# Causal grouped attention: the row maxima from the high halves alone, two heads at a time on rows 0-63 and 64-127 of the array, and the side work of a round placed anew

## What is computed

```python
q = (x @ wq).reshape(b, t, HQ, K)       # HQ = 16, K = V = 64
k = (x @ wk).reshape(b, t, HKV, K)      # HKV = 4, G = 4 query heads for each key head
v = (x @ wv).reshape(b, t, HKV, V)
q = q * cos + _neg_half(q) * sin
k = k * cos + _neg_half(k) * sin
qg = q.reshape(b, t, G, HKV, K)
scores = jnp.einsum('btghk,bThk->bghtT', qg, k)
scores = jnp.where(mask, scores, -jnp.inf) / np.float32(np.sqrt(K))
p = jax.nn.softmax(scores, axis=-1)
out = jnp.einsum('bghtT,bThv->btghv', p, v).reshape(b, t, HQ * V)
return out @ wo
```

## Time and profile before

| | us |
|---|---|
| median of 3 runs | 1379.15 (1377.59 to 1379.6) |
| the profiled execution | 1377.09 |
| its span, first to last instruction | 1375.3 |
| mean granted TensorE clock in the span | 0.921 |

### The profile page before, as it was taken

One profiled execution on the slowest core, in us unless ns is written; L12 is line 12 of the kernel. 1 busy time (PEld: TensorE's weight loads), 2 busy tenths in 40 slices (PEclk: granted clock), 3 DMA queues, 4 the chain that ended last, 5 costly groups with the idle time before them and its releaser, 6 DMA issues.

```text
span 1375.3 us, 35916 instructions
## 1 busy us (share of the span) xinstructions
PE 1123.1 (82%) x14984; PEld 841.2 (61%) x14984; DVE 1056.3 (77%) x2097; ACT 840.2 (61%) x1488; POOL 1000.7 (73%) x786
## 2 busy tenths in 40 slices
PE   4767776459999999999999999999999998610891
PEld 2666666126667676776676766767767676510781
DVE  5576665768889889888898898888988975583665
ACT  2644555258778787787787777877877886100230
POOL 2554567659888888898898888988988897317355
PEclk9999998579999999999999999999999999555896
DMA  6140001122122121122221211212212110013694
GB/s 210 41 142 1 1 2 68 41 88 52 54 67 49 50 74 37 51 59 55 59 52 46 74 36 54 57 55 58 52 47 48 36 26 1 1 35 116 193 301 153
DMA packets 49246, 90.84 MB, mean 66 GB/s; under 512 B 8896, under 2 KB 19136, under 8 KB 48832
## 3 DMA queue, kind: packets, MB, share of 16 engines
q1 hardware_dynamic: 46128, 81.21, 20.7%
q0 software_dynamic: 2960, 7.38, 1.9%
HBM read 43.96 MB, written 13.01 MB: 41 GB/s over the span
## 4 chain that ended last, share of the span: by engine, by line
PE 64%; DVE 19%; POOL 6%; issue 5%; SPq 3%; ACT 2%; DMA 1%; POOLq 0%; DVEq 0%
PE psT L1082 5%; PE psS L1152 5%; PE psS L1151 5%; PE psT L1070 5%; PE psS L1173 5%; PE psS L1174 5%; PE psS L1175 4%; PE psT L1100 3%; PE psO L1082 3%; PE psO L1152 3%; PE psO L1151 3%; POOL rows_in L708 2%; DVE pmax L1552 2%; DVE nmax L1401 2%; DVE psT L1529 2%
## 5 line engine op out<-in xcount | busy, mean ns | idle before, releaser
L682 POOL TENSOR_TENSOR probs<-arena,probs 128x512 f16<-128x512 f32 x576 | 652.3, 1157 | 113.5 <-ACT probs L866 113.1
L866 ACT ACTIVATE probs<-arena 128x512 f16<-128x512 f32 x576 | 358.0, 622 | 0.0
L874 ACT ACTIVATE arena<-psS 128x512 f32<-128x512 f32 x384 | 228.1, 594 | 144.7 <-PE psS L1155 82.4
L1173 PE MATMUL psS<-vb,probs 128*128 128x65 f16 x2304 | 301.9, 192 | 4.6 <-POOL probs L682 2.4
L1174 PE MATMUL psS<-vb,probs 128*128 128x64 f16 x2304 | 303.3, 194 | 0.0
L1175 PE MATMUL psS<-vb,probs 128*128 128x65 f16 x2304 | 301.4, 192 | 0.0
L1173 PEld LDWEIGHTS psS<-vb,probs 128*128 128x128 f16 x2304 | 220.0, 97 | 72.7 <-issue 9.4
L1174 PEld LDWEIGHTS psS<-vb,probs 128*128 128x128 f16 x2304 | 215.4, 97 | 47.4
L1552 DVE TENSOR_REDUCE pmax<-psT 128x1 f32<-128x512 f32 (+1 forms) x305 | 193.6, 639 | 39.7 <-PE psT L1082 19.0
L1175 PEld LDWEIGHTS psS<-vb,probs 128*128 128x128 f16 x2304 | 216.8, 98 | 0.0
L1152 PE MATMUL psS<-arena 65*128 65x512 f16 (+1 forms) x448 | 157.1, 351 | 0.0
(11 more groups left out here) (268 smaller groups left out, 2884.6 us busy)
## 6 DMA issues: line engine op xcount, KB each, us to landing
arena<-arena SPq DMA_DIRECT2D x240, 128.0 KB, 2.4
arena<-w_exp_dram SPq DMA_DIRECT2D x40, 384.0 KB, 4.2
arena<-xnT_d SPq DMA_DIRECT2D x16, 512.0 KB, 3.8
wkv<-w_d SPq DMA_DIRECT2D x16, 352.0 KB, 4.2
rows_in<-arena POOLq DMA_DIRECT2D x1, 2580.0 KB, 18.6
arena<-rows_in SPq DMA_DIRECT2D x40, 64.5 KB, 3.1
arena<-x_dram SPq DMA_DIRECT2D x4, 512.0 KB, 5.3
hres<-x_dram SPq DMA_DIRECT2D x4, 512.0 KB, 5.0
```

The lines of the kernel that those rows point to most:

```text
L682: pool.tensor_tensor(pl[:, r, :], pf[:, r, :], ph[:, r, :], ALU.subtract).then_inc(lo_P, 1)
L866: act.activation(ph[:, s % RING, :], pf[:, s % RING, :], ACT.Copy).then_inc(b_hi, 1)
L874: act.activation(pf[:, s % RING, :], score_banks[s % SCORES], ACT.Exp).then_inc(b_exp, 1)
L1173: pe.matmul(dst, high, vb[:, p, j, 0:OW], start=first, stop=False, skip_group_check=True)
```

## The change

The row maxima come from the high halves of q and k alone (K=64 instead of K=128). Two heads are done together: the matmul of head g reads qB and kB on partitions 0 to 63, that of head g+1 qA and kC on partitions 64 to 127, and they write two side banks; mask matmuls follow for both. So two "max" entries stand side by side in the list, and PE waits for both banks before it fills them. All maxima of heads 0 and 1 and five pairs for heads 2 and 3 are made in the round before, the other five pairs for heads 2 and 3 in steps 2 to 11 of the round. PROJ, OUTP, HIGH_AT, LOW_AT and the rows have new steps. The low halves of q for heads 0 and 1 count on a semaphore of their own (ql_in), for which scores of step 0 wait, no longer the maxima; qk_in therefore counts 112 a round. The first maxima of the next round's heads 2 and 3 (s = 31) wait for q1_in, which still counts all six copies. SP's order puts `spread_q(.., 0)` ahead of the rows, and there are two row semaphores. The prologue makes 30 maxima and two rows instead of 16 and one.

```diff
-EARLY = {4: (0,), 5: (1,), 6: (2,), 7: (3,), 8: (4, 5)}
-LATE = {0: (6,), 1: (7,), 2: (8,), 3: (9,)}
-ROW_AT = 5
+THIS_PAIR = {2: 5, 5: 6, 7: 7, 9: 8, 11: 9}
+NEXT_PAIR = {14: 0, 16: 1, 17: 2, 19: 3, 20: 4, 22: 5, 24: 6, 26: 7, 28: 8, 29: 9}
+LATER_PAIR = {31: 0, 32: 1, 33: 2, 34: 3, 35: 4}
+ROWS_AT = {13: 2, 15: 3, 31: 4, 33: 5}
...
-PROJ = {0: ("k", 0), 1: ("k", 1), 3: ("q", 0, 0), 5: ("r", 0, 0), 7: ("q", 0, 1), 9: ("r", 0, 1), 11: ("v",),
-        13: ("q", 1, 0), 15: ("r", 1, 0), 17: ("q", 1, 1), 19: ("r", 1, 1)}
-OUTP = {21: ("turn", 0), 23: ("turn", 1), 25: ("turn", 2), 27: ("turn", 3), 30: ("out", 0), 33: ("out", 1)}
-HIGH_AT = {4: 0, 12: 1, 22: 2}
-LOW_AT = {5: 0, 15: 1, 25: 2}
+PROJ = {0: ("k", 0), 1: ("k", 1), 3: ("q", 0, 0), 4: ("r", 0, 0), 6: ("q", 0, 1), 7: ("r", 0, 1), 9: ("v",),
+        16: ("q", 1, 0), 18: ("r", 1, 0), 21: ("q", 1, 1), 24: ("r", 1, 1)}
+OUTP = {11: ("turn", 0), 13: ("turn", 1), 15: ("turn", 2), 17: ("turn", 3), 20: ("out", 0), 23: ("out", 1)}
+HIGH_AT = {4: 0, 10: 1, 26: 2}
+LOW_AT = {5: 0, 11: 1, 27: 2}
...
+        if s in THIS_PAIR:
+            now += pair(2, THIS_PAIR[s])
+        if not last and s in NEXT_PAIR:
+            now += pair(G, NEXT_PAIR[s])
+        if not last and s in LATER_PAIR:
+            now += pair(G + 2, LATER_PAIR[s])
...
-                    sp.dma_start(qA[0:HD, p, 2 * c + h, :], qlo[HD * h:HD * h + HD, c, :]).then_inc(landed, 16)
+                    sp.dma_start(qA[0:HD, p, 2 * c + h, :], qlo[HD * h:HD * h + HD, c, :]).then_inc((ql_in, q1_in)[c], 16)
...
-                spread_row(row_of(1), p, 1)
                 if not last:
                     spread_k(it + 1, 1 - p)
+                    spread_q(it + 1, 1 - p, 0)
                 spread_row(row_of(2), p, 2)
-                if not last:
-                    spread_q(it + 1, 1 - p, 0)
                 spread_row(row_of(3), p, 3)
                 if not last:
                     spread_q(it + 1, 1 - p, 1)
                     spread_row(row_of(4), 1 - p, 0)
+                    spread_row(row_of(5), 1 - p, 1)
...
+            def fill_pair(e, banks, p, n):
+
+                g = e[1] % G
+                if g == 0 and e[2] == 0:
+                    pe.wait_ge(qk_in, 112 * n + 112)
+                if g == 2 and e[2] == 0:
+                    pe.wait_ge(q1_in, 96 * n + 96)
+                w = min(4, PIECES[e[2]][0][0] + 1 - 4 * PIECES[e[2]][0][1]) * P
+                done = []
+                for k, (i, h) in enumerate(PIECES[e[2]]):
+                    diag = h == i // 4
+                    mm = [pe.matmul(banks[0][:, k * w:(k + 1) * w], qB[0:HD, p, g, i * P:(i + 1) * P],
+                                    kB[0:HD, p, h * 512:h * 512 + w], start=True, stop=not diag),
+                          pe.matmul(banks[1][:, k * w:(k + 1) * w], qA[HD:P, p, g + 1, i * P:(i + 1) * P],
+                                    kC[HD:P, p, h * 512:h * 512 + w], start=True, stop=not diag)]
+                    if diag:
+                        mm = [pe.matmul(dst[:, (k + 1) * w - P:(k + 1) * w], identh[:, :], maskh[:, :],
+                                        start=False, stop=True) for dst in banks]
+                    done = mm
+                for mm in done:
+                    mm.then_inc(side_full, 1)
...
+                if e[0] == "max":
+                    before(entries, i + 1, base, prior)
+                    fill_pair(e, [side_banks[bank], side_banks[(i + 1) % SB]], (1 - p) if nxt else p, it + 1 if nxt else it)
+                    return
...
-                    pe.wait_ge(row_in, 16 * (it * G + g) + 16)
+                    pe.wait_ge(row_in[g % 2], 16 * (it * G + g) // 2 + (16 if g % 2 == 0 else 8))
+                if s == 0:
+                    pe.wait_ge(ql_in, 32 * it + 32)
```

More of the change, by code:

```diff
@@ L74, in reader, with pair @@
     return READER[entry[0]]
-PROJ = {0: ("k", 0), 1: ("k", 1), 3: ("q", 0, 0), 5: ("r", 0, 0), 7: ("q", 0, 1), 9: ("r", 0, 1), 11: ("v",),
-        13: ("q", 1, 0), 15: ("r", 1, 0), 17: ("q", 1, 1), 19: ("r", 1, 1)}
-OUTP = {21: ("turn", 0), 23: ("turn", 1), 25: ("turn", 2), 27: ("turn", 3), 30: ("out", 0), 33: ("out", 1)}
-HIGH_AT = {4: 0, 12: 1, 22: 2}
-LOW_AT = {5: 0, 15: 1, 25: 2}
+PROJ = {0: ("k", 0), 1: ("k", 1), 3: ("q", 0, 0), 4: ("r", 0, 0), 6: ("q", 0, 1), 7: ("r", 0, 1), 9: ("v",),
[3 more added lines that the diff above has]
+LOW_AT = {5: 0, 11: 1, 27: 2}
+def pair(h, n):
+    return [("max", h, n), ("max", h + 1, n)]
 def side_work(first, last):
@@ L88, in side_work @@
     for s in range(SPR):
-        h, c = divmod(s, SPH)
         now = []
[L91 to L94, removed]
+        if s in THIS_PAIR:
[4 more added lines that the diff above has]
+            now += pair(G + 2, LATER_PAIR[s])
         if not last and s in PROJ:
@@ L98, in side_work @@
             now.append(OUTP[s])
-        if c == ROW_AT and not (last and h == G - 1):
-            now.append(("row", h + 1))
+        if s in ROWS_AT and not (last and ROWS_AT[s] >= G):
+            now.append(("row", ROWS_AT[s]))
         steps.append(now)
@@ L106 @@
 SB = 3
-PROLOGUE = ([PROJ[s] for s in sorted(PROJ)] + [("max", G, n) for n in range(len(PIECES))] + [("row", G)]
-            + [("max", G + 1, n) for c in sorted(EARLY) for n in EARLY[c]])
+PROLOGUE = ([PROJ[s] for s in sorted(PROJ)] + [e for n in range(len(PIECES)) for e in pair(G, n)]
+            + [("row", G), ("row", G + 1)] + [e for s in sorted(LATER_PAIR) for e in pair(G + 2, LATER_PAIR[s])])
 PROLOGUE += [("gap",)] * (-len(PROLOGUE) % SB)
@@ L359, in build @@
         r_mul, r_hi, r_lo, qk_in = sem("rotated_parts"), sem("high_halves"), sem("low_halves"), sem("qk_in")
-        max_ready, row_in = sem("max_ready"), sem("row_in")
-        q1_in = sem("second_heads_in")
+        max_ready, row_in = sem("max_ready"), [sem("row_in0"), sem("row_in1")]
+        q1_in, ql_in = sem("second_heads_in"), sem("first_heads_low_in")
         b_hi, lo_P, v_hi = sem("high_probs"), sem("low_probs"), sem("high_values")
@@ L457, in spread_row @@
                 sp.dma_start(qB[HD:HD + 1, p, g, :].rearrange("o (i t) -> o i t", t=P),
-                             hrow[:, g % 2, :]).then_inc(row_in, 16)
+                             hrow[:, g % 2, :]).then_inc(row_in[g % 2], 16)
             for b in range(2, B):
@@ L482, in _ @@
             store_input2(2)
-            spread_row(start(0, "A"), 0, 0)
+            spread_row(1, 0, 0)
+            spread_row(2, 0, 1)
             store_input2(3)
@@ L1072, in fill @@
                     return mm
[L1073 to L1087, removed]
                 if kind == "row":
@@ L1123, in side @@
                 e = entries[i]
-                if e[0] == "gap":
+                if e[0] == "gap" or e[0] == "max" and e[1] % 2 == 1:
                     return
@@ L1196, in _ @@
                     pe.wait_ge(ones_set, 4)
-                if PROLOGUE[i] == ("max", G + 1, 0):
+                if PROLOGUE[i] == ("max", G + 2, 0):
                     pe.wait_ge(n2_T, 2)
```

## The result

The changed kernel takes 1546.7 us (median of 4 runs, 1545.47 to 1552.85) against 1378.37 us: a ratio of 1.1233, with a 95% interval of 1.1198 to 1.1268. The forecast was 1455 and the range ended at 1510: the direction was right, the size less than half of what came (+77 forecast, +168 measured).

The account below looks back on a forecast made before the run. PE's stream was taken to bound the old round; the new round, walked along DVE, was 59.0 us against 54.4. 1377.1 + 69 (fifteen rounds) + 10 (prologue) - 2 (last round) = 1454, median 1455, range 1385 to 1510.

Parts of the forecast that it names:

- The stalls: PE waiting for copies of q before the next round's first maxima: 5.5 us at s 31, 1.7 at s 14.
- The chain of s 31: From DVE's read of r(1,1) through ACT, POOL and SP copies until q1_in lands: 10.3 us, plus 0.5 to DVE's read.
- Rival C: Mild: ACT and POOL run ahead, chains 2 to 3 us shorter; 55 to 56.6 us a round, 1395 to 1420; chance 0.10.
- rival B: Faster: array halves work, landings come in time, DVE is next; 50 to 52.5 us a round, 1320 to 1360; chance 0.11.
- the price of a change of form: PE entering and leaving the half-array form, some 48 times a round: about 0.03 us each, 1.5 us a round.
- The bound above, 0.17: Upper bound per change of form, from a 512-column matmul's pipeline beyond its streaming (0.38 - 0.21): 8 us a round.
- The saving of the halves: Main matmuls of the maxima side by side on rows 0-63 and 64-127 cost half: 3.9 us a round less.
- the clock: Lower PE clock after the 5.5 us stall, from s 31 to 35: up to 1.5 us, counted only in the range.
- The walk of DVE: Round summed leg by leg along DVE: 59.0 us against 54.4; PE's own walk gave 59.4, or 57.9 without array changes.
- Ends: Prologue with 30 maxima instead of 16: +10 us; last round with 10 maxima instead of 24 gives back 2.
- A: Clock and array: halves run serially or each change costs 0.17, clock counts in full; 1495 to 1560; chance 0.20 with D.
- D: The halves run one after the other, so the array change does nothing: 61.8 us a round, 1498; chance 0.20 with A.

Follow-up runs that it names:

- e3: Kernel before the change, its maxima as matmuls on rows 0 to 63 one head after another, nothing packed, 96 changes of array form a round; 1522.45 us.
- e5: e1 with both heads of a pair on rows 0 to 63, so no two matmuls lie side by side; 1530.45 us.
- e1: Changed kernel with the low copies of q for heads 2 and 3 on their own semaphore, so the maxima at s 31 wait only for high copies; 1484.55 us.
- e2: Changed kernel with 72 filler matmuls of 128 columns before the wait for q1_in at s 31, to keep PE busy; 1541.83 us.
- e7: e1 with pairs 0, 1, 2 of the next round at s 16, 17, 18 instead of s 14, 16, 17; 1470.51 us.

## Why the prediction was right in sign and short in size

**The stalls were right.** At s 31 I had 5.5 us, measured 4.8; at s 14 1.7, measured 1.5; the old bank waits 1.4, now 1.9. Sum 8.6 forecast, 8.2 measured. The chain of s 31 was to be 10.3 us long from DVE's last read of r(1,1); it is 10.6, from 747.55 to 758.16. Its links on ACT, POOL and SP's queue (SPq), in the changed kernel:

```profile
748.59 1.06 ACT L848 ACTIVATE arena<-arena 128x1024 f16<-128x1024 f32 x1
```

```profile
750.73 2.28 POOL L689 TENSOR_TENSOR probs<-arena,probs 128x512 f16<-128x512 f32 x2 [0.68 <-ACT probs L873]
752.97 2.12 POOL L662 TENSOR_TENSOR arena<-arena 128x1024 f16<-128x1024 f32 x1
```

```profile
755.12 1.10 SPq L459 DMA_DIRECT2D arena<-arena  x2
```

DVE's last read starts at 746.86 and takes 0.69. ACT starts 1.0 us after it (0.9 forecast). From there to POOL's end of the low half it is 755.09 - 748.59 = 6.5 us, 6.45 in the sum, though not by its terms: POOL begins 2.1 us after ACT, not 3.2, and does two subtractions before the low half, not one. PE goes on 3.0 us after the first copy's issue (2.95). Rival C, which had the chain shorter, and rival B, whose landings come in time, fall with that.

**The failed step is the price of a change of form,** "the nearest row, a K=65 matmul behind a K=128 one, shows no gap, so I take about 0.03, 1.5 us a round". It is 0.10 (e3), 4.9 us a round. The row was near in its number of rows, but it is the full-array form, so it did not hold the thing that was to be priced. The bound above, 0.17, had it inside. The saving of the halves is 3.5 us (e5), not 3.9. So where I had the array give 3.9 - 1.5 = 2.4 us a round, it takes 4.9 - 3.5 = 1.4.

**The second is the clock.** I let it cost up to 1.5 us in the forecast's own range and nothing in its middle, because its low stretch would fall where DVE sets the pace. In the 4.1 us at 0.50 PE is busy 4.13: it sets the pace there, not DVE. PE's stream is 1.8 us longer by it (56.7 in the changed kernel, 54.9 in e1); 0.6 of that comes back, because the waits for banks are 1.9 us in place of e1's 2.5. A round is 1.2 us longer by it (e2).

**The walk of DVE was the wrong walk to sum.** Its legs were 12.9, 8.2, 18.9, 10.8, 8.2; measured 13.1, 8.8, 21.7, 11.2, 10.1. The legs up to s 14 and the stall are within 0.6; the two that went wrong are those in which PE had more to do than DVE: s 14 to s 24 with seven pairs and 16 changes, PE busy 20.4 of 21.7 us and DVE 17.8; and s 31 to the next k(0) with the low clock, PE 9.6 of 10.1 and DVE 6.6.

**Small errors in the sums.** The columns are written at 0.21/512 us each but were multiplied at about 0.215/512: the scores come to 16.8 us and not 17.2, the maxima to 7.6 and not 7.7. POOL's start, 716.99 to 719.76 less 0.5, is 2.3 us and not 2.15. None of them decides anything.

The round, once more, from the terms as measured: stream before 53.2, halves -3.5, 48 changes +4.9, the stream's part of the clock 1.8, waits 8.2: 64.6, against 64.94 in this round; 0.3 us is not assigned. Over 15 rounds the miss was (10.7 - 4.6) x 15 = 92 us, 6.1 a round: array 3.8, the stream's part of the clock 1.8, waits -0.4, PE's walk instead of DVE's 0.4, and 0.5 that is not assigned (two rounds with more of the low clock, 66.7 and 67.5 us, are among it).

**Ends.** The prologue was +13.6 instead of +10. In it each pair waits for DVE because of the one-entry reserve, at half the clock:

```profile
294.34 0.58 PE L1107 MATMUL psO<-arena 64*128 64x512 f16 x1 [0.77 <-DVE pmax L1574]
...
295.79 0.58 PE L1107 MATMUL psT<-arena 64*128 64x512 f16 x1 [0.84 <-DVE pmax L1572]
```

I had 2 us for this in front of the first scores; eight such waits, of 0.50 to 0.88 us, stand between 294 and 313 us, 6.0 us in all. The last round gave back 0.3, not 2.

**The rivals.** A gave 1495 to 1560 and holds the measured time, but by luck, since neither of its two causes came: the halves do not run one after the other (D with it), and a change does not cost 0.17. What came is the forecast's mechanism with a dearer change and the low clock that A warned of: PE idle for 4.84 us is followed by 4.1 us at 0.50, while the waits of 1.5 us and less in this round are not (in e1 and e2 waits of 1.9 to 2.8 us were, in some rounds). It would by itself have moved the forecast by 1.2 x 15 = 18 us. The Trainium skill (TensorE: Matmul & The Clock Gate, Why this matters for your kernels) warns against idle gaps between bursts of matmuls, and the trace agrees at these 4.84 us.

What would have taken the change to the break-even: without the stall at s 31, e1, it is at 1485; with pairs later as well, e7, at 1471. No paired version that was run comes near the kernel before.

## What to carry to other kernels

Two half-array matmuls side by side save one matmul's streaming, 0.21 us for 512 columns, but in this kernel the way into the half form and out of it cost 0.10 us each; so one pair between full-array matmuls gains nothing at 512 columns and loses below. Collect several pairs behind one change, or leave it (several pairs at a time was not tried here; it needs more free banks). Before moving the reader of a copied operand forward, count the chain behind the copy to its landing, low-priority parts too, and give each consumer a semaphore for just the parts that it reads: that alone was 62 us here. And when two walks of a round come out near each other, price the terms that only one of them contains before taking either.

## What the runs showed of the hardware that I had not expected

- A change between full-array and 64-row matmuls costs 0.10 us each way at the full clock (96 of them lengthen PE's stream by 9.8 us a round). At a change the weight load does not run ahead of the matmul before (701.28 and 701.60), while between two half-array matmuls on the same rows it does (892.24 for 892.46). A matmul on 65 rows has no gap behind one on 128 (692.89 to 693.11).
- Matmuls on rows 0-63 and 64-127 start within 0.01 us of each other and are listed with the same length; this saved 3.5 of 3.9 us.
- A stall of 4.8 us in each round costs, beyond itself, 1.2 us: 4.1 us of PE's work at half the clock, of which one half, 2.1 us, would be the most. In e2, with the stall filled by matmuls, the clock still fell in five of fourteen rounds, behind waits of 2.1 to 2.7 us at s 14 in three of them and of 1.5 us at s 31 in two.
